# GpSimd takes over the subtraction that splits a head's merged weights (layer 0)

## The reference, cut to what matters

```python
q_c = hidden_size @ Wq_c.T + bq_c                         # 192 wide
q = (q_c @ Wq_up.T + bq_up).reshape(b, s, NH, Q_HEAD)     # 32 heads of 128 + 64
kv = hidden_size @ Wkv_c.T + bkv_c                        # 64 latent + 64 rope
kvu = (kv_nope @ Wkv_up.T + bkv_up).reshape(b, s, NH, QK_NOPE + V_HEAD)
k = concatenate([k_nope, k_rope])
attn = softmax(einsum('bhqd,bhkd->bhqk', q, k) / sqrt(Q_HEAD))
o = einsum('bhqk,bhkv->bhqv', attn, v)
out = einsum('bhsv,Hv->bsH', o, Wo) + bo
x = layernorm(x + out)
```

## Time and profile before

| | us |
|---|---|
| median of 3 runs | 1416.69 (1416.06 to 1417.42) |
| span of the profiled execution | 1414.5 |
| TensorE busy | 1400.8 (99%) |
| VectorE busy | 1017.2 (72%) |
| ScalarE busy | 891.0 (63%) |
| GpSimd busy | 773.5 (55%) |

### The profile page before, as it was taken

One profiled execution on the slowest core, in us unless ns is written; L12 is line 12 of the kernel. 1 busy time (PEld: TensorE's weight loads), 2 busy tenths in 40 slices (PEclk: granted clock), 3 DMA queues, 4 the chain that ended last, 5 costly groups with the idle time before them and its releaser, 6 DMA issues.

```text
span 1414.5 us, 30207 instructions
## 1 busy us (share of the span) xinstructions
PE 1400.8 (99%) x8769; PEld 1237.2 (87%) x8769; DVE 1017.2 (72%) x2528; ACT 891.0 (63%) x2445; POOL 773.5 (55%) x828
## 2 busy tenths in 40 slices
PE   9999999999999999999999999999999999999998
PEld 8888889888788878889889889889889889889886
DVE  5999999999968875665665665665665665665776
ACT  5888888888555576556556565556556556556721
POOL 3555555555040367765765765665665665665521
PEclk9999999999999999999999999999999999999999
DMA  5533333322445301111001001001011101000201
GB/s 197 168 96 95 95 94 95 93 67 50 134 135 163 98 31 60 32 31 59 30 30 59 30 30 59 30 30 59 30 30 59 30 30 59 30 30 30 83 20 42
DMA packets 56155, 92.60 MB, mean 65 GB/s; under 512 B 6064, under 2 KB 27312, under 8 KB 56112
## 3 DMA queue, kind: packets, MB, share of 16 engines
q1 hardware_dynamic: 55968, 91.93, 21.5%
q10 hardware_dynamic: 144, 0.13, 0.0%
HBM read 81.82 MB, written 2.10 MB: 59 GB/s over the span
## 4 chain that ended last, share of the span: by engine, by line
PE 93%; DVE 3%; ACT 1%; issue 1%; DMA 1%; POOL 1%; SPq 0%; POOLq 0%; DVEq 0%; ACTq 0%
PE c_bv L106 8%; PE c_bv L108 7%; PE c_bv L107 7%; PE h_bo L947 5%; PE c_bx L106 5%; PE c_bx L108 4%; PE c_bx L107 4%; PE c_by L106 4%; PE c_by L108 4%; PE c_by L107 4%; PE h_bt L75 3%; PE a_acc L1450 3%; PE h_bo L1450 3%; PE h_bs L106 2%; PE c_bt L75 2%; PE h_bs L108 2%
## 5 line engine op out<-in xcount | busy, mean ns | idle before, releaser
L621 POOL TENSOR_TENSOR h_pr<-h_pr,h_rinv 128x512 f32<-128x512 f32 x128 | 133.3, 1041 | 136.5 <-DVE h_rinv L772 134.2
L1781 POOL TENSOR_TENSOR c_qk<-g_y,c_qk 128x512 fp32r<-128x512 f32 x96 | 124.0, 1292 | 146.3 <-ACT c_qk L1893 139.6
L1632 POOL TENSOR_TENSOR b_sw_lo<-b_slots,b_sw_hi 128x512 fp32r<-128x512 f32 (+1 forms) x128 | 148.1, 1157 | 10.2
L1630 POOL CAST b_sw_hi<-b_slots 128x512 fp32r<-128x512 f32 (+1 forms) x128 | 72.7, 568 | 144.5 <-DMA b_slots<-in_w_qk 125.2
L106 PE MATMUL c_bv<-b_wv_hi,g_xT_hi 128*128 128x256 f32 x496 | 138.8, 280 | 0.2 <-DVE g_xT_lo L1186 0.2
L108 PE MATMUL c_bv<-b_wv_hi,g_xT_lo 128*128 128x256 f32 x496 | 138.8, 280 | 0.0
L107 PE MATMUL c_bv<-b_wv_lo,g_xT_hi 128*128 128x256 f32 x496 | 138.7, 280 | 0.0
L2002 DVE TENSOR_TENSOR c_bo<-c_bo,g_wo 128x128 f32<-128x128 f32 x128 | 38.3, 299 | 122.2 <-ACT g_wo L1868 117.6
L1893 ACT ACTIVATE c_qk<-g_y 128x512 fp32r<-128x512 f32 x96 | 60.7, 632 | 96.4 <-DVE g_y L2039 67.1
L674 ACT ACTIVATE h_pr<-h_bs,h_nmax 128x256 f32<-128x256 f32 x256 | 119.4, 480 | 2.5 <-DVE h_nmax L767 2.4
L1858 ACT ACTIVATE c_pr<-c_pr,c_rinv 128x128 f32<-128x128 f32 (+1 forms) x256 | 101.9, 448 | 9.0 <-DVE c_rinv L1992 9.0
(11 more groups left out here) (480 smaller groups left out, 5141.9 us busy)
## 6 DMA issues: line engine op xcount, KB each, us to landing
f_wi<-in_w_ffn SPq DMA_DIRECT2D x66, 256.0 KB, 2.7
b_slots<-in_w_qk SPq DMA_DIRECT2D x64, 256.0 KB, 3.0
a_w<-in_w_head SPq DMA_DIRECT2D x28, 352.0 KB, 2.9
h_part<-in_w_ffn SPq DMA_DIRECT2D x32, 264.0 KB, 2.7
b_raw_v<-in_w_v SPq DMA_DIRECT2D x16, 512.0 KB, 4.5
b_raw_o<-in_w_o SPq DMA_DIRECT2D x16, 512.0 KB, 4.6
h_o_mix<-h_o_hi SPq DMA_DIRECT2D x62, 128.0 KB, 2.2
b_ffn_w<-in_w_ffn SPq DMA_DIRECT2D x4, 576.0 KB, 5.5
```

What stands on the lines that cost most here:

```text
L621: pool.tensor_tensor(pr[b][:, :, :], pr[b][:, :, :], rinv[b][:, :][:, :, None].to_broadcast([P, 2, S]), ALU.mult)\
L1632: pool.tensor_tensor(self.sw[1][:, a:b], self.slots[:, a:b], f32(self.sw[0][:, a:b]), ALU.subtract)\
L1781: pool.tensor_tensor(lo, src, f32(hi), ALU.subtract).then_inc(s_sumlo, 1)
```

## The change

The low part of the merged weights is subtracted by GpSimd and no longer by VectorE, for heads 2 to 31. GpSimd does it in the same odd round, first thing behind its `scaled`, behind a wait for `s_ghi`, and it signals `s_glo`. VectorE's `merged_lo` stays for heads 0 and 1.

```diff
@@ GpSimd's program
+                def merged_lo(h):
+                    hi, lo = merged_weights(h)[0]
+                    pool.wait_ge(s_ghi, h + 1)
+                    pool.tensor_tensor(lo[:, :, :], gm[:, :, :], f32(hi[:, :, :]), ALU.subtract).then_inc(s_glo, 1)
+
                 def round_(h, b):
                     s = 4 * h + b
                     if has(s - 1, NS) and not (isinstance(s, int) and s == 1):
                         scaled(s - 1, (b - 1) % 4)
+                    fresh = merged_next(h, b - 1)[0] if b % 2 else None
+                    if is_late(fresh):
+                        merged_lo(fresh)
                     if isinstance(h, int):
                         lat.add_bias(pool, h, b)
@@ VectorE's round_
                     if b % 2 and has(2 * h - 2 + b // 2, NPAIR):
                         outs(2 * h - 2 + b // 2, b // 2)
-                    if is_late(fresh):
-                        merged_lo(fresh)
                     if has(s - 2, NS):
                         probs(s - 2, (b - 2) % 4)
```

## The result

The changed kernel takes 1420.86 us (median of 7 runs, 1420.27 to 1424.47) where the kernel before takes 1416.69 (median of 7, 1415.88 to 1417.45): 4.2 us more. The ratio is 1.0033, with a 95% interval of 1.0024 to 1.0042. The span of the profiled execution grew from 1414.5 to 1419.0 us.

What follows compares the result with a forecast made beforehand. TensorE, busy 1400.8 of 1414.5 us, was taken as the bound; 25 turns at 0.19 us (4.75) plus 0.55 for the other heads gave 5.3 us more, 1422.0 us, range 1418 to 1427.

Steps and rivals of the forecast that it cites:

- a margin of some 0.12 us: Ahead of TensorE's query product: VectorE's subtraction is ready 0.17 us before its user, 0.12 with the time of a signal.
- Duration on GpSimd: The moved subtraction takes 0.74 us on GpSimd, against 0.407 on VectorE; bounds 0.73 and 1.19.
- Wake-up: GpSimd, idle and waiting for a semaphore, starts the subtraction 0.08 us after ScalarE's rounding ends.
- (c): GpSimd takes the subtraction up slowly or is held: 1431.6 us, or 1435.5 with a 1.19 us operation; chance 0.06.
- Signal: TensorE's weight load for the query product starts 0.05 us after GpSimd's subtraction ends.
- The wait of one head: TensorE's query-product load moves from 202.97 to 203.16, a 0.19 us wait; 4.75 us over 25 loop turns.
- Head 2 and the four last: Heads outside the loop, where the wait is 0.11 us each: 0.55 us in all.
- The delayed split of the value weights: In two of the last heads, GpSimd's split runs some 0.9 us later: put at nothing, upper bound 0.15 us twice.
- VectorE's relief at nothing: Taking 30 subtractions, 12.2 us busy time, off VectorE gains 0, since the next instruction, L776, follows ScalarE.
- Rival (a): TensorE's 0.31 us "issue" gap each loop turn shrinks by the added stall: no change, 1416.7 us; chance 0.11.
- Rival (b): VectorE was the hidden bound, so removing its subtractions makes it faster, at most 12.2 us, 1404.5; chance 0.03.
- The other signs: Profile signs: 30 GpSimd subtractions (26 and 4) of 0.74 us; loop turn 10.33 us instead of 10.14.

Runs made afterwards that it cites:

- late_wait: Changed kernel, with TensorE's query product waiting for the low part only ahead of its third matmul, the first that reads it: 1415.78 us, ratio 0.9995.
- half_gpsimd: Changed kernel, with GpSimd subtracting only 2 x 64 of the 2 x 128 columns for heads 2 to 27: 1416.55 us, ratio 1.0002.
- twice_vector: Kernel before, with VectorE making the subtraction twice, the second waiting for the first, and GpSimd nothing: 1427.36 us, ratio 1.0077.
- relief: Kernel before, with VectorE subtracting only 2 x 8 of the 2 x 128 columns for heads 2 to 27: 1416.60 us, ratio 0.9999.

## Why the prediction was right, point by point

- *Direction and size.* Forecast 5.3 us more, 1422.0 (1418 to 1427); measured 4.2, 1420.86. The mechanism, a margin of some 0.12 us that the slower engine overdraws, is the one that late_wait, half_gpsimd and twice_vector show; the forecast was 1.1 us too high.
- *Duration on GpSimd.* Taken 0.74 from the same form in another stage; measured 0.734 (median of 26, 730 to 740 ns). The ratio of 1.96 of the Trainium skill ("GPSIMD Engine Reference", section 3.1) would have made it 0.80, an estimate; measured is 0.734 to 0.407, 1.8.
- *Wake-up.* 0.08 us taken; 204.79 to 204.87 is 0.08. The rival of a slow wake-up or a held GpSimd (c) falls: no subtraction took longer than 0.741 us. In a round with the split of the value weights outside the loop GpSimd's next scaling started 0.08 us behind L615's end (315.22 to 315.30), so following L615 isn't what makes the 0.40 of the earlier trace rows. That the end of a turn of the loop makes it fits, and isn't shown.
- *Signal.* 0.05 us taken; 205.61 to 205.65 is 0.04.
- *The wait of one head.* 0.19 taken, 0.17 measured in the timeline and 0.164 in the turn. This is the term that was mis-sized, by 25 x 0.026 = 0.6 us of the 1.1 by which the forecast was high. Three differences of up to 0.01 us make it up (the chain ahead of GpSimd was 1.33 us instead of 1.34, the operation 0.734 instead of 0.74, the signal 0.04 instead of 0.05), which is about as fine as these records can be read. The other 0.5 is no step of the forecast: 0.2 is the unchanged rest of the kernel, which came out shorter in the profiled execution, and 0.3 lies between the spans, which differ by 4.5, and the medians, which differ by 4.2.
- *Head 2 and the four last.* 0.11 us each taken, 0.55 in all; measured some 0.56. In the first of the last four, the load came at 308.57 behind one at 308.35, 0.22 where the pace is 0.115: 0.1. The delayed split of the value weights cost nothing: the scaling behind it ended at 316.34, and the turn's load followed at 316.55, not waiting. This scaling, put at 311.3 instead of 310.92, was hardly late itself: it started 4.38 us after its time before (315.30), where the whole timeline had moved by about 4.4.
- *VectorE's relief at nothing.* Right: relief took 1416.60 us, and L784 starts 0.03 us behind ScalarE in the changed kernel.
- *Rival (a), the "issue" gap takes it back.* Fell: the gap is 0.3 us in both kernels, and the delay of a load goes fully into the turn at both sizes. *Rival (b)* fell with L784, which starts no sooner, and with relief.
- *One reading announced was wrong.* The list of waits was to show the query's load waiting for GpSimd some 28 times at 0.2 us. It doesn't appear at all; only the distances between the loads show it. In twice_vector, at 0.33 us, it does appear, 26 times. The other signs came true: 30 subtractions of 0.74 us (26 and 4), and a turn of 10.30 us where 10.33 was announced.

## What to carry to other kernels

An operation may go to a slower engine when its result has a margin at its reader. In this kernel the price was not its busy time but its overdraft: (new end + signal) - (the reader's start today), each time, because nothing behind the reader took it back. Before moving work, look at the first instruction that reads it: here one wait stood in front of five matmuls of which only the third and the fifth read the low part. Moving two matmuls to the front gained 4.1 us on the kernel before, about what the change of the engine had cost, and with them in front the engine made no measurable difference. Relief for an engine that runs behind another one's output became idle time here; the instruction behind the removed one, and what released it, tells this in its rows.

## What the runs showed of the hardware

VectorE held GpSimd up where both read two inputs from SBUF at once: GpSimd's 128x256 subtraction took 0.956 us beside VectorE's subtraction of the same size (0.41 us, begun 0.05 us earlier, not lengthened) and 0.735 us beside one of 0.16 us. The Trainium skill, "SBUF — State Buffer", section Who interferes with whom, says that a VectorE instruction with two inputs in SBUF contends with a GpSimd instruction that reads SBUF, and that the order of issue decides which of them blocks. The trace agrees on both, for the one order that was run: GpSimd, the later one, pays. The amount, 0.22 us, is less than the 0.36 us by which the two records overlap. This didn't touch the change itself: there the subtraction is made only once and took 0.730 to 0.741 us. A version in which the two engines share it wasn't run.
